# Look-ups of the relation stage: one column a chunk, each behind the landing of the last

## The reference

```python
seg = edge_type * n + dst
agg = segment_sum(x[src], seg, num_segments=34 * n)
mean = agg.reshape(34, n, -1) / jnp.maximum(cnt, 1.0).reshape(34, n, 1)
h1 = einsum('rni,rio->no', mean, W_rel) + x @ W_root + b_rgcn
```

## Time and profile before

| | us |
|---|---|
| three runs, median (lowest to highest) | 2742.63 (2736.82 to 2745.43) |
| profiled execution, span from first to last instruction | 2894.8 |
| TensorE busy (share of the span) | 2439.6 (84%) |
| VectorE busy | 1510.0 (52%) |
| ScalarE busy | 1062.8 (37%) |
| GpSimd busy | 939.9 (32%) |
| relation stage, from the first to the last gather of h rows | 611.1 to 1752.2 |
| sum stage, from the first to the last gather of messages | 1777.4 to 2092.2 |

### The profile page before, as it was taken

The page is one execution under the profiler, slowest core; times in us unless marked ns, Lnnn a source line. Parts: engine busy times, 40 slices in busy tenths (PEclk is TensorE's granted clock), DMA queues, the critical chain, the costliest instruction groups (busy, mean ns, idle before and its releaser), DMA issues.

```text
span 2894.8 us, 50550 instructions
## 1 busy us (share of the span) xinstructions
PE 2439.6 (84%) x13014; PEld 2255.6 (78%) x13015; DVE 1510.0 (52%) x2625; ACT 1062.8 (37%) x1833; POOL 939.9 (32%) x1172
## 2 busy tenths in 40 slices
PE   3777579778999998899999998778878879977799
PEld 1455579777888888888888887566777879977799
DVE  6655575643333333333333334777745687687534
ACT  3222322323333333333333333555522245446421
POOL 4766001134444444444444444767600000000000
PEclk9999899989999999999999988889989989989899
DMA  6000103554544545555455444777711110011102
GB/s 209 1 0 0 50 3 136 192 173 158 163 158 162 166 162 165 166 163 163 158 168 164 166 160 169 239 230 219 220 71 53 68 38 0 11 44 54 55 11 97
DMA packets 119791, 346.43 MB, mean 120 GB/s; under 512 B 30791, under 2 KB 31771, under 8 KB 119685
## 3 DMA queue, kind: packets, MB, share of 16 engines
q1 hardware_dynamic: 75221, 205.21, 20.3%
q0 software_dynamic: 44528, 140.69, 16.1%
HBM read 258.18 MB, written 91.47 MB: 121 GB/s over the span
## 4 chain that ended last, share of the span: by engine, by line
PE 60%; DVE 12%; issue 9%; another core or an unknown queue 8%; ACT 5%; DMA 3%; DVEq 2%; POOL 1%; ACTq 1%; POOLq 0%; SPq 0%
PE ps L1530 38%; PE ps L1587 10%; PE ps L1521 5%; PE ps L1657 4%; PE ps L1731 2%; DMA land<-messages,stage 1%; DVE xw L1487 1%; DVE h_act L1113 1%; DVE w_a L1036 1%; ACT land L859 1%; DVE land L1172 1%; DVE land L1432 1%; ACT agg_w L829 1%; DVE land L1126 1%
## 5 line engine op out<-in xcount | busy, mean ns | idle before, releaser
L1530 PE MATMUL ps<-w_a,h_t 128*128 128x384 f32 x4968 | 951.4, 347 | 32.4 <-issue 28.6
L1530 PEld LDWEIGHTS ps<-w_a,h_t 128*128 128x128 f32 x4968 | 893.7, 195 | 50.1 <-issue 45.4
L1587 PE MATMUL ps<-xw,agg_w 128*128 128x384 f32 x2800 | 533.0, 352 | 108.7 <-DVE agg_w L1135 71.2
L1587 PEld LDWEIGHTS ps<-xw,agg_w 128*128 128x128 f32 x2800 | 517.4, 198 | 121.4 <-issue 109.3
L1436 DVE TENSOR_TENSOR h_t<-ps,h_t 128x256 fp32r<-128x256 f32 x408 | 169.8, 423 | 706.3 <-ACT h_t L967 585.5
L1530 PE MATMUL ps<-xw,h_t 128*128 128x384 f32 x2448 | 492.4, 357 | 27.7 <-issue 27.7
L1530 PEld LDWEIGHTS ps<-xw,h_t 128*128 128x128 f32 x2448 | 458.0, 200 | 38.2 <-issue 37.9
L967 ACT ACTIVATE h_t<-ps 128x256 fp32r<-128x256 f32 x408 | 153.2, 383 | 744.3 <-PE ps L1530 287.7
L679 POOL DMA_INDIRECT h_act<-h_table,stage x139 | 147.5, 1061 | 509.2 <-DVE land L1432 485.2
L1521 PE MATMUL ps<-ident,land 128*128 128x128 f32 x1176 | 184.2, 299 | 95.8 <-DVE land L1432 48.6
L1521 PEld LDWEIGHTS ps<-ident,land 128*128 128x128 f32 x1176 | 152.7, 154 | 118.4 <-DVE h_t L1436 56.4
(11 more groups left out here) (224 smaller groups left out, 2121.7 us busy)
## 6 DMA issues: line engine op xcount, KB each, us to landing
land<-in_L_gnn_W_rel SPq DMA_DIRECT2D x198, 384.0 KB
messages<-land SPq DMA_DIRECT2D x136, 384.0 KB
land<-x_state SPq DMA_DIRECT2D x40, 384.0 KB, 3.0
messages<-land POOLq DMA_DIRECT2D x34, 384.0 KB, 2.6
land<-in_L_gnn_W SPq DMA_DIRECT2D x10, 1152.0 KB
x_state<-land SPq DMA_DIRECT2D x30, 384.0 KB, 2.3
adj<-x_state SPq DMA_DIRECT2D x10, 384.0 KB
h_act<-x_state SPq DMA_DIRECT2D x1, 3840.0 KB
```

The costliest lines, as they stand in the source:

```text
L1530: ins = pe.matmul(acc(h), h_t[:, a, k, :], w[:, b, k, h * HF:(h + 1) * HF], start=(k == 0 and a == 0 and b == 0), stop=(stop and k == KB - ...
L1587: ins = pe.matmul(ps[:, 2 + 2 * u + h, 0:wide], agg_w[:, a, b, :], xw[:, c, b, h * HF:h * HF + wide], start=first, stop=last, skip_group_c ...
```

## The change

GpSimd's loop of the relation stage issues its five columns of look-ups in other steps. Before: columns 0 and 1 in the step k = 0, 2 and 3 in k = 1, 4 in k = 2, none in k = 3. Now: 0, 1 and 2 in one step each and 3 and 4 in k = 3. Ahead of every column but the first stands a wait until the column before has landed in full (both its DMAs, 32 counts of `R.col_got`).

```diff
                     if k == 0:
                         pool.wait_ge(R.col_addr, i + 1)
                         pool.sem_inc(turn_taken, 1)
-                    for m in ((0, 1), (2, 3), (4,), ())[k]:
+                    for m in ((0,), (1,), (2,), (3, 4))[k]:
+                        if m > 0:
+                            pool.wait_ge(R.col_got, 32 * PER * i + 32 * m)
+                            pool.sem_inc(turn_taken, 1)
                         look_up(m)
```

## The result

| | us |
|---|---|
| before, 20 runs, median (lowest to highest) | 2737.25 (2724.7 to 2745.43) |
| changed, 20 runs, median (lowest to highest) | 2712.21 (2698.31 to 2738.91) |
| ratio, 95% interval | 0.9903 (0.9886 to 0.9921) |
| span of the profiled execution, before and after | 2894.8 and 2716.6 |

The change makes the kernel 1.0% faster: 2737.25 x (1 - 0.9903) = 26.6 us. The profiled execution of the changed kernel has a time of its own, 2718.22, so 1.6 us lie around its span.

A forecast was written before the change was run, and what follows sets the result against it. TensorE's chunks were taken as bound, delayed where dense look-ups meet the matrix load: 182.3 us lost profiled, less 152.2 for recording, leaves 30.1; 2742.6 - 30.1 = 2712.5, range 2683 to 2735 (45%).

The forecast's parts named there:

- the stall that the prediction reads: Relation stage: 4.0 us in a relation's chunk while eight look-ups meet the matrix load; with clock echo 182.3 us in all.
- Where the stage loses time: Relation stage: profiled chunks take 8.44 us against 6.965 undisturbed, losing 182.3 us, about 5.9 a relation.
- The signs that were to show it right: Profile after: ScalarE's "remote" waits under 60 us, turns about 7 us, clock nearly 1.00, span down 100 us or more.
- Part (a): GpSimd issues four look-ups, not eight, during the matrix load; the stall goes, up to 182.3 us of the profiled execution.
- So recording made the program at least 152.2 us longer: Whole program: profiled span 2894.8 less timed median 2742.63, put down to the profiler's recording, likeliest in the stall.
- Rival 1: Relation stage: the stall exists only where DMAs are recorded; timed median stays at 2735 to 2750; chance 29%.
- The timed runs lose 30.1: Relation stage: 182.3 us of profiled loss less 152.2 of recording leaves 30.1 us lost in timed runs, all gained.
- (b): GpSimd's added waits for columns 1 and 2 cost nothing: 6.9 us between columns, a look-up lands in 2.38.
- (c): GpSimd's fourth step adds 6.0 us; its round is 21.8 us, 3.5 of it waits, under 27.9 of four chunks.
- Rival 3: GpSimd's round becomes the bound if look-ups land slowly, 31.2 us a round at 7.1: slower, 2825 us; chance 12%.

The follow-up runs named there:

- e10b: Kernel before, unaltered, traced on a chip of the first kind (kernel before about 2735 us): one run of 2714.42 us, span 2712.8.
- e5: Kernel before with SyncE's relief (it waits for a store's landing only ahead of the next store, ScalarE waits itself), second kind of chip (about 2891): 2898.18 us, ratio 1.0019.
- e6: Changed kernel's look-up places without its waits for landings, plus SyncE's relief, second kind of chip: 2714.18 us, ratio 0.9403 to the kernel before.
- e12: Repeat of e5 (kernel before with SyncE's relief), again on the second kind of chip: 2892.89 us, ratio 1.0007.
- e11: Repeat of e6 (spread look-ups without waits, SyncE's relief), again on the second kind of chip: 2719.86 us, ratio 0.9401.
- e8: Kernel before with columns 0, 1 in the third step and 2, 3, 4 in the fourth, no waits, plus SyncE's relief, second kind: 2859.62 us, ratio 0.9917.
- e4: Kernel before, each matrix piece loading only 8 of 768 columns, look-ups unchanged, first kind of chip: 2676.07 us, ratio 0.9786.
- e1: Changed kernel's look-up places without its waits for landings, against the kernel before, first kind of chip: 2739.35 us, ratio 1.0012.
- e9b: Changed kernel, unaltered, run again against the kernel before on a chip of the first kind: 2710.91 us, ratio 0.9886.
- e2: Kernel before's look-up places with a wait for the column before ahead of each, first kind of chip: 2788.26 us, ratio 1.0189 to the kernel before.
- e7: Changed kernel, spread and waits, plus SyncE's relief, second kind of chip: 2728.54 us, ratio 0.9425 to the kernel before.
- e3: Kernel before with columns 0, 1 in the third step and 2, 3, 4 in the fourth, off the matrix load, no waits, first kind: 2684.71 us, ratio 0.9826.

## Why the prediction came out as it did

The time was forecast at 2712.5 and is 2712.21. That this fits is luck. The loss was put at 30.1 us, all of it to be gained; it is 58.5, of which 26.6 are gained and 31.9 stay. And what the change acts on in the runs of the result is not the stall that the prediction reads.

**Where the stage loses time: right for the chip of the trace, and not tested by the result.** The signs that were to show it right all came (no wait for "remote", turns at 7 us, a clock of 1.00, a span down by 178.2), but e10b shows nearly the same (7.18 us a chunk, with bouts) with the look-ups unchanged, so they tell the chips apart and not the kernels. Part (a) itself holds on the second kind of chip: e5 and e6 differ in the spread alone and take 8.46 and 7.12 us a chunk, and e12 and e11 repeat it. The matrix load is no needed part of it: in e8 SyncE issued only stores in the stretch shown, and the DMA engines were 0.13 busy.

**"So recording made the program at least 152.2 us longer": wrong, the step that failed.** The timed runs were of a chip of the first kind, and the trace has all the marks of one of the second: the span of 2894.8 is within 0.2% of the 2890.62 and 2891.73 measured there, and e5 and e12 show the same waits in the same numbers. Which chip made the trace is not recorded, so this is inferred. Rival 1, and the rule of the Trainium skill weighed for it ("NOTIFIC — the notification-queue block", 7.1 Overflow), do not explain the 152.2: e10b, recorded in full, took 2714.42, less than any run beside it, and e5's traced run of 2899.96 lies among its other eleven. That recording has a part in the stall on the second kind alone is not excluded, since every run there was recorded in some measure. What lies around the span is 1.6 us, not the 9 to 15 that I drew from the Trainium skill ("Runtime: NRT & Kernel Launch", the ~15µs preamble/postamble breakdown).

**"The timed runs lose 30.1": mis-sized, and another mechanism.** It is 58.5 by e4: bouts in which a store's landing comes late to SyncE, ScalarE waits at its copy out, and SyncE's chain of stores and matrix pieces bounds the stage. The forecast's spread alone does not cure that: e1 has it and gains nothing, and SyncE's chain bounds it nearly throughout. With the waits too, the store landings that SyncE waits for take 2.68 us in place of 3.20, ScalarE waits 9.0 us in place of 61.0, and the bound passes to GpSimd's chain at 7.13 us a chunk. Why the waits shorten the landings is not shown. In e10b they take 2.68 as well (316.5 us in 118 waits), and its time is within the spread of the changed kernel's; the 26.6 stand in the medians, and no trace of a typical, slower run of the kernel before shows where it has them.

**(b) "The added waits for columns 1 and 2 cost nothing": wrong.** It took the landing of one lone look-up, 2.38 us, and GpSimd in step with the copies. In the changed kernel 94 waits took 190.1 us from 689 to 1540, some three a round at 2.02 each, up to 4.3. GpSimd has fallen behind for nearly the whole stage and goes through its rounds at its own pace; its steps are some 5 us apart in the round shown, not 6.9, so the column before has less time to land.

**(c) The round of GpSimd: mis-sized.** 21.8 us was forecast, 3.5 of it waits; the round shown has 26.75, of which 0.94 + 1.26 + 3.47 + 0.38 = 6.05 are waits for look-ups, and longer ones exceed four undisturbed chunks, so that VectorE waits for GpSimd (14.0 us; 30.4 in e9b by the same line from 689 to 1600). A late gather was to wait for nobody; but the stage also ends with GpSimd's look-ups, and there its delay costs some 11 us at once, a term that the sum did not have. Rival 3's mechanism is thus at work inside the gain, and in e2 it decides: 1.0189.

Open: how much SyncE's relief gives on the first kind of chip, since the run with it never came to one, and with it a version that has neither bound. Open too is what on the chip holds back TensorE and ScalarE in the stall, and why one kind of chip has it. The changed kernel itself was not run on the second kind; e7, which has the relief besides, suggests some 5.7% there.

None of the versions is best everywhere. On the first kind e3 leads (0.9826); its look-ups with the relief give only 0.9917 on the second. On the second kind e6 (0.9403, 0.9401 in e11) and e7 (0.9425) are not clear of each other, and neither was run on the first.

## What to carry to other kernels

Where a profiled span and the timed runs disagree by more than the spread of either, look for another chip before blaming the profiler: run the unchanged kernel with a trace beside its own timed runs. And compare the traces of before and after only when they come from the same kind of chip. When small DMAs are taken apart in time, cost the waits at the landing under load, not at that of a lone transfer, and check that the issuing engine's round, waits included, stays well under the round of the engine that bounds the stage. Once it falls behind, every wait that was covered lengthens its round, and the next stage may have to wait for it as well. To see what bounds a stage, follow the chain that ended last through the stage's window alone. A serial queue of stores and loads, each behind a landing, can be such a bound. Putting the small DMAs where it has no load due gave 1.7% on the first kind of chip (e3), but with the relief only 0.8% on the second, where they must be apart (e8 against e6).

## What the runs showed of the hardware that was not expected

- The same program took 2735 us on two chips and 2891 on a third (in two comparisons there), 5.7% apart. The difference goes with one pattern, eight look-up DMAs of 128 four-byte words each within 12 us (ten in 15 us in e8). Without it (e6, e11) the third chip took 2714.18 and 2719.86.
- In that stall ScalarE and VectorE started nothing for 4 us, and matmuls came singly, 0.7 us apart, with the DMA engines 0.13 busy (e8).
- GpSimd's wait for a look-up's landing was 2.38 us where it ran alone, and up to 5.6 us in the stage, with gathers, stores and loads going on (e7).
